# Block inverses in four parts instead of two; preparation of the filter stage moved into the projection

## The reference, cut to what matters

```
q, k, v = silu(causal 4-tap convolution of x @ W.T)           # 4 heads of 64
beta    = sigmoid(x @ Wb.T)
A       = strictly lower part of -(beta k)(k^T), in chunks of 32 tokens
T       = inverse(I - A)                                      # 32 x 32, 64 chunks x 4 heads x 4 batches
local_s, local_m, local_l = causal filters of v with 3, 15 and 63 taps
probs   = softmax((x @ gate_w + gate_b) / temp) * (1 - 5 eps) + eps     # 5 gates a head
o       = p0 local_s + p1 local_m + p2 local_l + p3 delta(q, k, v, T) + p4 v
```

## Time and profile before

| | us |
|---|---|
| median of three runs | 2339.09 (2338.53 to 2339.15) |
| the profiled execution | 2325.58 |
| its span | 2323.8 |
| projection | 0 to 359.15 |
| filter stage | 359.15 to 576.40 |
| delta stage and network | 576.40 to 2323.8 |

### The profile page before, as it was taken

One profiled execution on the slowest core, in us unless ns is written; L12 is line 12 of the kernel. 1 busy time (PEld: TensorE's weight loads), 2 busy tenths in 40 slices (PEclk: granted clock), 3 DMA queues, 4 the chain that ended last, 5 costly groups with the idle time before them and its releaser, 6 DMA issues.

```text
span 2323.8 us, 41398 instructions
## 1 busy us (share of the span) xinstructions
PE 2086.2 (90%) x16936; PEld 1766.6 (76%) x16936; DVE 1157.7 (50%) x1819; ACT 864.5 (37%) x1406; POOL 533.1 (23%) x563
## 2 busy tenths in 40 slices
PE   7888873776899888779999999999999999999998
PEld 5776763676777777658888888888888888888886
DVE  5777768963477767732343244234324323432332
ACT  4445541110233333234344344434434433443442
POOL 1112787875455554500000000000000000000000
PEclk9999996798799999989999999999999999999999
DMA  5766666776999999500000000000000000000000
GB/s 162 203 189 178 185 206 173 245 248 235 217 226 207 208 206 204 132 27 1 19 19 1 19 19 1 19 19 19 1 19 19 1 19 19 19 1 19 19 1 18
DMA packets 247007, 217.02 MB, mean 93 GB/s; under 512 B 159042, under 2 KB 210754, under 8 KB 242242
## 3 DMA queue, kind: packets, MB, share of 16 engines
q1 hardware_dynamic: 234562, 184.30, 31.0%
q10 hardware_dynamic: 12288, 30.41, 4.5%
HBM read 130.52 MB, written 84.15 MB: 92 GB/s over the span
## 4 chain that ended last, share of the span: by engine, by line
PE 55%; issue 1%; DVE 1%; ACT 1%; DMA 0%; POOL 0%; DVEq 0%; SPq 0%; ACTq 0%; POOLq 0%
PE B L1573 49%; PE O L1600 5%; PE T L1531 1%; DVE yb L1706 0%; ACT gate L1645 0%; DMA x<-x_s 0%; DVE stats L1737 0%; ACT L1645 0%; DVE z L1732 0%; DVE z L1728 0%; DVE xl L1686 0%; DVE z L1751 0%; ACT xh L1633 0%; POOL rstd L1787 0%; DVEq L1701 0%
## 5 line engine op out<-in xcount | busy, mean ns | idle before, releaser
L1573 PE MATMUL B<-act1l,wr 128*128 128x512 f32 x1024 | 398.5, 389 | 0.0
L1573 PE MATMUL B<-act0h,wr 128*128 128x512 f32 x1024 | 398.3, 389 | 0.0
L1573 PE MATMUL B<-act0l,wr 128*128 128x512 f32 x1024 | 398.3, 389 | 0.0
L1573 PE MATMUL B<-act1h,wr 128*128 128x512 f32 x1024 | 398.3, 389 | 0.0
L1659 ACT ACTIVATE yb<-B,scol 128x512 f32<-128x512 f32 x256 | 176.2, 688 | 581.1 <-PE B L1573 581.1
L1694 DVE TENSOR_TENSOR act0l<-yb,act0h 128x512 fp32r<-128x512 f32 x256 | 176.1, 688 | 378.0 <-ACT act0h L1662 375.8
L1784 POOL TENSOR_TENSOR rstd<-mv,ln_eps 128x4 f32<-128x4 f32 x16 | 3.2, 199 | 1303.5 <-DVE mv L1745 1303.5
L453 DVE SCALAR_TENSOR_TENSOR acc<-proj,taps,acc 128x512 f32<-128x512 f32 x288 | 214.7, 750 | 84.8 <-ACT acc L399 76.3
L1694 DVE TENSOR_TENSOR act1l<-yb,act1h 128x512 fp32r<-128x512 f32 x128 | 88.7, 693 | 295.4 <-ACT act1h L1662 295.4
L1573 PEld LDWEIGHTS B<-act0h,wr 128*128 128x128 f32 x1024 | 192.3, 188 | 39.9
L1573 PEld LDWEIGHTS B<-act1h,wr 128*128 128x128 f32 x1024 | 192.3, 188 | 39.9
(11 more groups left out here) (169 smaller groups left out, 3213.7 us busy)
## 6 DMA issues: line engine op xcount, KB each, us to landing
qk_s<-yT SPq DMA_DIRECT2D x16, 1024.0 KB, 6.2
kk_s<-kfull SPq DMA_DIRECT2D x16, 1024.0 KB, 6.4
qk<-qk_s SPq DMA_DIRECT2D x32, 512.0 KB, 6.5
wraw<-in_ffn_w ACTq DMA_DIRECT2D x32, 352.0 KB, 6.5
toe<-in_toe_short ACTq DMA_DIRECT2D x32, 320.0 KB, 7.4
xt<-in_xt SPq DMA_DIRECT2D x16, 524.0 KB, 4.3
k_s<-ktok SPq DMA_DIRECT2D x16, 512.0 KB, 7.2
v_s<-vtok SPq DMA_DIRECT2D x16, 512.0 KB, 3.2
```

The lines of the kernel that those rows point to most:

```text
L1573: last = nc.tensor.matmul(B[slot % 4][:, :], w, part, start=(k == 0 and i == 0), stop=(k == kts - 1 and i == len(parts) - 1))
```

## The change

The matrices are inverted in four parts of four steps each, two slots of `tri` a part. GpSimd does parts 0 to 2: part 0 in its iterations 6 to 9, part 1 in 10 to 13, part 2's columns 1 to 24 in 14 to 16 and the rest in the filter stage. VectorE does part 3 in the filter stage, 60 operations spread over groups 4 to 51. The scale tables of parts 0 to 2 are made behind steps 4, 8 and 12 and turned in steps 5, 9 and 13, and with them three quarters of the gates' softmax: logits behind steps 4, 8 and 12, shares behind steps 5, 9 and 13. The three engines' loops over steps are unrolled. The first head's windows are written from the value tile in each step, SBUF to SBUF; the first three band matrices are loaded at the program's start, and the zeros in them are set there. In the filter stage the remaining quarter is prepared, the first two convolutions come ahead of it, the softmax's table ahead of the block table, and the query scales behind the third weighing. The inverses leave in four parts, through two transposed tiles in turn.

```diff
-NSUB = GRP // P
-EARLY_STEPS = STEPS // NSUB
-
-EARLY_COLS = {10: (1, 5), 11: (5, 9), 12: (9, 12), 13: (12, 15), 14: (15, 18), 15: (18, 21), 16: (21, 25)}
+
+PARTS = 4
+PART_STEPS = STEPS // PARTS
+PSLOTS = SLOTS // PARTS
+PGRP = GRP // PARTS
+
+EARLY_COLS = {6: (0, 1, 8), 7: (0, 8, 14), 8: (0, 14, 20), 9: (0, 20, 31),
+              10: (1, 1, 8), 11: (1, 8, 14), 12: (1, 14, 20), 13: (1, 20, 31),
+              14: (2, 1, 8), 15: (2, 8, 15), 16: (2, 15, 25)}
 EARLY_END = 25
...
-    first = t * NS % P
+    c = t // PART_STEPS
+    if c >= 2 and t % PART_STEPS == 0:
+        queue.wait_ge(keep["tri_in"][c % 2], c // 2 * 16 * NQ * PART_STEPS)
     for q in range(NQ):
-        queue.dma_start(keep["tri"][first:first + NS, q * NSUB + t // EARLY_STEPS, :, :],
+        first = q // 2 * PGRP + t * NS % PGRP
+        queue.dma_start(keep["tri"][first:first + NS, c * PSLOTS + q % 2, :, :],
                         io["kk_s"][q * CH:q * CH + CH, t * NS:t * NS + NS, q * CH:q * CH + CH].rearrange("i n j -> n i j")
-                        ).then_inc(keep["tri_in"][t // EARLY_STEPS], 16)
+                        ).then_inc(keep["tri_in"][c % 2], 16)
+
+
+def blocks_there(engine, keep, c):
+    engine.wait_ge(keep["tri_in"][c % 2], (c // 2 + 1) * 16 * NQ * PART_STEPS)
...
+                    sp.dma_start(win0[:, NT + t * BATCH:NT + (t + 1) * BATCH, :], vtok[p][:, 0, :, :]).then_inc(v_stored[p], 16)
+                    sp.dma_start(win0[WIN:P, t * BATCH:(t + 1) * BATCH, :], vtok[p][0:WIN, 0, :, :]).then_inc(v_stored[p], 16)
+                    if t + 1 < STEPS:
+                        sp.dma_start(win0[0:WIN, (t + 1) * BATCH:(t + 2) * BATCH, :], vtok[p][WIN:P, 0, :, :]).then_inc(v_stored[p], 16)
...
-                    early = isinstance(t, int) and t == EARLY_STEPS + 1
+                    c = t // PART_STEPS - 1
+                    early = c in range(PARTS - 1) and t % PART_STEPS == 1
                     if early:
-                        pe.wait_ge(gam0_done, 1)
-                        nc.tensor.transpose(gam_ps, gam0[:, :, :, :].rearrange("p t r s -> p (t r s)"), ident).then_inc(gam0_turned, 1)
+                        pe.wait_ge(gam0_done, c + 1)
+                        turn_scales(nc, gam_ps, gam0, ident).then_inc(gam0_turned, 1)
                     turn(lambda hh, b: yT[p][:, KT + hh, b * P:b * P + P]).then_inc(ktok_ready, 1)
                     if early:
-                        pe.wait_ge(gam0_out, 2)
+                        pe.wait_ge(gam0_out, 2 * c + 2)
...
+                for t in range(STEPS):
...
+                for n in range(NTOE):
+                    toeplitz(act, io, keep, n)
+                act.wait_ge(prm_in, 16)
+                nc.scalar.activation(itemp[:, :], prm[:, NGATE:NGATE + HEADS], ACT.Exp, scale=-1.0).then_inc(itemp_done, 1)
...
+                for t in range(1, STEPS):
+                    step(t, t % 2, (t - 1) // 2, True, t < 2)
+                    if t % PART_STEPS == 0:
+                        c = t // PART_STEPS - 1
+                        act.wait_ge(small_out, t + 1)
+                        if c:
+                            act.wait_ge(gam0_done, c)
+                        nc.scalar.activation(ebeta[:, :, :], raw[:, c * NE:c * NE + NE, NGATE:NGATE + HEADS], ACT.Exp,
+                                             scale=-1.0).then_inc(exp0_done, 1)
+                        act.wait_ge(to_exp0, c + 1)
+                        nc.scalar.activation(lg0[:, :, :, :], lg0[:, :, :, :], ACT.Exp).then_inc(exp0_done, 1)
...
+                def first_logits(c):
+                    if c == 0:
+                        link(nc.vector.tensor_scalar(eps[:, :], prm[:, NGATE + HEADS:NGATE + 2 * HEADS], 0.0, 0.2, ALU.max, ALU.min))
+                        link(nc.vector.tensor_scalar(slope[:, :], eps[:, :], -5.0, 1.0, ALU.mult, ALU.add))
+                        dve.wait_ge(itemp_done, 1)
+                    dve.wait_ge(small_out, (c + 1) * PART_STEPS + 1)
+                    gate_logits(nc, link, keep, lg0, mx0, rows(c)).then_inc(to_exp0, 1)
+
+                def first_shares(c):
+                    dve.wait_ge(exp0_done, 2 * c + 2)
+                    link(gate_shares(nc, link, keep, lg0, mx0, rows(c)))
+
+                def first_scales(c):
+
+                    dve.wait_ge(kk_summed, (c + 1) * PART_STEPS + 2)
+                    nc.vector.tensor_scalar(ssk0[:, :, :].rearrange("p (t b) h -> p t (b h)", b=BATCH),
+                                            kk[:, c * PART_STEPS:(c + 1) * PART_STEPS, :], L2_EPS, None, ALU.add)
+                    dve.wait_ge(exp0_done, 2 * c + 1)
+                    link(nc.vector.tensor_scalar(ebeta[:, :, :], ebeta[:, :, :], 1.0, None, ALU.add))
+                    link(nc.vector.tensor_tensor(half0[:, :, :], ssk0[:, :, :], ebeta[:, :, :], ALU.mult))
+                    link(nc.vector.reciprocal(half0[:, :, :], half0[:, :, :]))
+                    if c:
+                        dve.wait_ge(gam0_turned, c)
+                    by_matrix(nc, gam0, half0[:, :, :]).then_inc(gam0_done, 1)
...
+                    if t % PART_STEPS == 0:
+                        first_logits(t // PART_STEPS - 1)
+                        first_scales(t // PART_STEPS - 1)
+                    if t % PART_STEPS == 1 and t > 1:
+                        first_shares(t // PART_STEPS - 1)
...
+                        c, first, end = EARLY_COLS[t]
+                        sub = Substitution(nc.gpsimd, keep, c, keep["outer0"])
                         if first == 1:
...
+                            pool.wait_ge(gam0_out, 2 * c + 2)
+                            pool.wait_ge(keep["sub_link"], c * SUB_LINKS + 1)
                             sub.scaled_columns().then_inc(keep["sub_link"], 1)
...
+                            pool.wait_ge(keep["sub_link"], c * SUB_LINKS + 2)
                             sub.ones_on_diagonal()
...
+                        early_columns(pool, sub, keep, c, first, end)
+                        if end == CH - 1:
+                            early_rows(pool, sub, keep, c)
+                    if t % PART_STEPS == 1 and t > 1:
+                        c = t // PART_STEPS - 1
+                        if c < PARTS - 1:
+                            blocks_there(pool, keep, c)
+                            Substitution(nc.gpsimd, keep, c, None).zero_above().then_inc(keep["sub_link"], 1)
...
+SUB_LINKS = 2 + 2 * (CH - 2)
...
+def early_columns(pool, sub, keep, c, first, end):
     for j in range(first, end):
...
+        pool.wait_ge(keep["sub_link"], c * SUB_LINKS + 2 * j)
         sub.outer_product(j).then_inc(keep["sub_link"], 1)
...
+        pool.wait_ge(keep["sub_link"], c * SUB_LINKS + 2 * j + 1)
         sub.update(j).then_inc(keep["sub_link"], 1)
+
+
+def early_rows(pool, sub, keep, c):
+    pool.wait_ge(keep["sub_link"], (c + 1) * SUB_LINKS)
+    sub.scaled_rows().then_inc(keep["inv_done"][0], 1)
+
+
+def gate_logits(nc, link, keep, lg, mx, rows):
+
+    temp = bcast(bcast_mid(keep["itemp"][:, :], rows.stop - rows.start), 5)
+    link(nc.vector.tensor_tensor(lg[:, :, :, :].rearrange("p t h f -> p t (h f)"), keep["raw"][:, rows, 0:NGATE],
+                                 bcast_mid(keep["prm"][:, 0:NGATE], rows.stop - rows.start), ALU.add))
+    link(nc.vector.tensor_tensor(lg[:, :, :, :], lg[:, :, :, :], temp, ALU.mult))
+    lgf = lg[:, :, :, :].rearrange("p t h f -> p (t h) f")
+    link(nc.vector.tensor_reduce(mx[:, :], lgf, AX.X, ALU.max))
+    return nc.vector.tensor_tensor(lgf, lgf, bcast(mx[:, :], 5), ALU.subtract)
+
+
+def gate_shares(nc, link, keep, lg, mx, rows):
+
+    n = rows.stop - rows.start
+    lgf = lg[:, :, :, :].rearrange("p t h f -> p (t h) f")
+    link(nc.vector.tensor_reduce(mx[:, :], lgf, AX.X, ALU.add))
+    link(nc.vector.reciprocal(mx[:, :], mx[:, :]))
+    by_head = mx[:, :].rearrange("p (t h) -> p t h", h=HEADS)
+    link(nc.vector.tensor_tensor(by_head, by_head, bcast_mid(keep["slope"][:, :], n), ALU.mult))
+    link(nc.vector.tensor_tensor(lgf, lgf, bcast(mx[:, :], 5), ALU.mult))
+    return nc.vector.tensor_tensor(keep["pw"][:, :, :, rows].rearrange("p h f t -> p t h f"), lg[:, :, :, :],
+                                   bcast(bcast_mid(keep["eps"][:, :], n), 5), ALU.add)
+
...
+def turn_scales(nc, out, gam, ident):
+
+    for rows in HALVES:
+        last = nc.tensor.matmul(out[rows, :], gam[rows, :, :, :].rearrange("p t r s -> p (t r s)"), ident[rows, rows],
+                                start=True, stop=True)
+    return last
...
+        OPS = 2 * (CH - 2)
+        SUB_END = 4 + OPS * 4 // 5
+
+        D_OUT, T_OUT = {2: 0, 6: 1, 12: 2, 28: 3}, {4: 0, 8: 1, 14: 2, 29: 3}
+
+        TURNS = {2: 0, 5: 1, 11: 2, 27: 3}
...
+                pe.wait_ge(keep["toe_zero"], NTOE)
                 convolve(0)
                 convolve(1)
+                pe.wait_ge(gam_done, 1)
+                turn_scales(nc, gam_ps, gam, ident).then_inc(gam_turned, 1)
...
```

(102 more changed lines are left out.)

218 lines of the change are left out of this document (57 added, 161 removed).

## The result

The changed kernel takes 2390.66 us (median of 4 runs, 2377.91 to 2398.22); the kernel before took 2338.81 (4 runs, 2328.75 to 2339.15). The ratio is 1.0227, interval 1.0175 to 1.0279: 52 us slower, where 13 us faster were forecast. On the two chips used further down the kernel before took 2324.61 and 2323.91 us, so kernels are compared by their ratio to it on the same chip. The profiled execution took 2389.58 us, with a span of 2387.6.

The account below looks back on a forecast made before the run. Bounds: in projection a TensorE, ScalarE and VectorE loop; in the heads VectorE (first), DMA (third), TensorE's pace (fourth). Projection +39 and filter stage -52 gave -13 us, so 2326 us; range 2303 to 2344.

Parts of the forecast that it names:

- The inverses' 6.3 MB leave in four parts: Filter stage heads: two parts leave in head 1, one each in heads 2 and 4, priced at 311 GB/s.
- points at steps 4, 8, 12: Projection: three preparation points on VectorE instead of one, with waits for GpSimd at 8 and 12; about +13 us.
- turns and shares, 5, 9, 13: Projection: scale tables turned in three steps instead of one (+6), softmax ended behind the last convolution (+6); about +12 us.
- GpSimd late, steps 10 and 14: Projection: GpSimd some 5 us late at the squares VectorE awaits, 0.8 us each; 1.5 us in all.
- tail: Projection's end: ten columns instead of four follow GpSimd's last key squares, and the stage waits for them; +11.5 us.
- the lock: Steps 8 and 12: VectorE operations each wait for one GpSimd operation of about 1.1 us; 5.2 us of waiting a point.
- Preparation of the filter stage: Filter stage's start: softmax shrinks to a quarter, first weighing after 14 us instead of 35.7; about -21 us.
- The four heads: Filter stage after the first weighing: 36 + 40.5 + 33.5 + 32.5 = 142.5 us against 174.2; about -31 us.
- (b): Filter stage: transfers don't scale with bytes, window bursts ahead of filter matrices stall TensorE; 2345 us, chance 0.10.
- (a): Projection from step 6 on: GpSimd becomes the pace, seen at squares of steps 10, 14 and the end; 2356 us, chance 0.14.
- (c): Projection: preparation points cheap, no lock at steps 8 and 12, GpSimd ends 8 late; +18, 2305 us, chance 0.16.
- (d): Filter stage: transfers give way, heads run at TensorE's pace of 28.2 us; 2298 us, chance 0.10.

Follow-up runs that it names:

- the split version: The changed kernel with each of its twelve 512 KB inverse stores issued as two, 64 rows outermost: 2307.13 us, ratio 0.993; run again 2309.06 us, ratio 0.9928.
- the quiet version: The split version with GpSimd's columns moved out of steps 8 and 12 to the steps beside them: 2304.06 us, ratio 0.9926.

## Why the prediction was wrong

**The failed step: "The inverses' 6.3 MB leave in four parts ... At 311 GB/s".** I priced the stores by bytes at the rate of all sixteen engines. They ran on two, at 53 GB/s. Forecast for the stage 165 us, measured 250.8; with the stores on sixteen engines 169.1. Of the 86 us between forecast and result 82 go with the form of these stores alone. The diff had all that was needed: `"q n (i j)"` puts a size of two outermost. I looked at bytes and piece sizes, which had not changed, and not at the shape.

**Projection, +39 forecast, +30.85 measured.** Token loads after (SyncE, start and length), the ones around steps 8 to 10:

```profile
188.34 0.35 SPq L235 DMA_DIRECT2D xt<-in_xt  x1
215.12 0.35 SPq L235 DMA_DIRECT2D xt<-in_xt  x1
236.80 0.35 SPq L235 DMA_DIRECT2D xt<-in_xt  x1
257.76 0.35 SPq L235 DMA_DIRECT2D xt<-in_xt  x1
```

| term | forecast | measured, from the token loads unless said |
|---|---|---|
| start | +3 | +3.75 (first product 13.45 against 9.70) |
| points at steps 4, 8, 12 | +13 | +12.5: 22.26, 26.78 and 26.38 us against 3 x 20.3, less 2.0 |
| turns and shares, 5, 9, 13 | +12 | +2.7: 23.20, 21.68, 21.67, less the 3.0 of before |
| GpSimd late, steps 10 and 14 | +1.5 | +1.3: 20.96, 20.97 (the latter from the v_s stores) |
| tail | +11.5 | +12.0: GpSimd ends 18.5 us behind the last v_s store (371.44 to 389.96), before 6.5 |
| unrolled loops | -2 | about -1: a plain step is 20.18 and no longer alternates |

The one term that is far off is the turns and shares: at steps 9 and 13 they cost 1.4 us each and not 5.5. The table is one trace, though. In the second trace of the split version, whose projection has the same code, the steps at the points took 23.87, 27.75 and 26.51 us and those of the turns 23.22, 25.05 and 21.65, so by it the points cost 15.2 and the turns and shares 6.0. Even there the latter are half the forecast. That GpSimd's end closes the projection was right, and the length of its tail from the fit over sizes came out within half a microsecond.

At steps 8 and 12 the sum was right and its parts were not. VectorE's gap is 6.25 us (200.06 to 206.31), not 8.5, and the quiet version's is 3.5 (204.60 to 208.12): the point's own work is about the 3.3 of the forecast, and the lock 2.7 instead of 5.2. The rest came from TensorE. Its timeline in the changed kernel at step 8, then a stretch behind the point, and one behind the same point in the second trace of the split version:

```profile
206.12 1.36 PE L331 MATMUL side<-yT 64*128 64x128 f32 x16 [3.97 <-ACT kfull L407]
208.67 3.86 PE L293 MATMUL proj<-xt,w_qkv 128*128 128x262 f32 x8 [1.19 <-DVE acc L470]
```

```profile
207.00:213.00 6.00, 4.82 (x24) 3.25 (x22) 3.71 (x6) 3.43 (x5) 0.00 (x0) 0.50 0.00 0
```

```profile
209.00:221.00 12.00, 10.94 (x80) 8.87 (x81) 5.72 (x10) 3.90 (x6) 3.48 (x2) 0.50 0.20 50
```

TensorE has no work for 3.97 us, until 206.12. From 207 its granted clock is 0.50, the lower of its two levels (1.2 and 2.4 GHz), and it is back at 1.00 in the slice that begins at 214. The eight products that took 2.03 us at 200.12 take 3.86 at 208.67. I had no term for that. In the second trace the pause is the same (3.98 us) and the lower level lasts for more than 12 us, although TensorE is busy for 10.94 of them; the next step, which begins at that level, is 25.05 us long where it was 21.68. A tensor-by-scalar operation does wait for GpSimd, as the prediction took it to (1.09 us against 0.19), but for less than a whole GpSimd operation, and the next one, at 204.03, not at all (0.18 against 0.20). The rule that I took this from (the Trainium skill, SBUF — State Buffer, Who interferes with whom) agrees with these rows; my price of it was too high.

**Preparation of the filter stage, -21 forecast.** Right: 12.4 us to the first weighing, where 14 was said and 11 to 20 allowed.

**The four heads, -31 forecast.** With split stores the heads take 34.2, 40.9, 43.7 and 29.8 us (first weighing at 402.46, then the rows of that kernel), forecast 36, 40.5, 33.5 and 32.5: 148.5 for 142.5. The second term that was mis-sized is the third head. It was to fall from 42.87 to 33.5 us because an inverse's bytes leave it, and it stayed: 11.9 MB at 273 GB/s (273 x 43.65) where 10.2 MB at 311 was forecast. The second trace has 44.1 us at 270 GB/s. Why full engines moved less there is open.

So with split stores the two stages come to +31 and -48, or -17 us, in the first trace and to +36 and -46, or -10, in the second; the timed ratio of 0.993 is -16 us, and I had said -13. The first trace as a whole is 28 us shorter than that of the kernel before, but 11 of these lie in the later stages, whose code is the same. The number would have been near by luck in part: the projection was 8 us cheaper in that trace than forecast and the third head 10 us dearer. The idea of the change held for a kernel that this one was not.

**The rivals.** (b) was nearest: the transfers don't scale with bytes, a burst stalls TensorE. But its mechanism (windows ahead of filter matrices, 2345 us) is not what cost the 82 us; a head as long as its 42.9 us did come with split stores, but only one, the third (43.7). (a) fell where it was priced, since steps 10 and 14 were no later than forecast; in the last steps GpSimd is indeed full, and there its length was in my sum. (c) was right in that the lock was cheap, but the points still cost 12.5 us and GpSimd's tail 12.0. (d) fell, with split stores: heads 2 and 3 stand at 40.9 and 43.7 us with full DMA engines. No rival had a transfer that is confined to a part of the engines, so the range ended 47 us too low.

## What to carry to other kernels

For each transfer that a change reshapes, write down the outermost size of both of its sides before its bytes: with the same 4 KB pieces an outermost size of two ran at 53 GB/s and four at 105, and with 64 the low plateau was gone and the stage 82 us shorter. In a trace, look for stretches where a DMA share stands still at a low value and the rate with it while nothing else runs: 0.13 here. Such a store also holds up other work: every transfer with a share on its engines, and every issue behind it in its queue, waits. Here each of the twelve lengthened the stage by 6.6 to 7.3 us. Four to six microseconds in the projection could be argued over for a page, and one `rearrange` outweighed them all.

Before a step's length is explained from one trace, look at a second one of the same kernel: here one ended its projection 5 us later than the other.

## What the hardware showed that I had not expected

- A store on two engines delays transfers that have all sixteen: the stage's last 2 MB store landed 24.8 us after its issue behind such stores and 6.3 us without them. SyncE's queue was held for up to 15 us at a 512 KB issue.
- A full DMA share does not fix the rate: 0.99 went with 316 GB/s in one head and 1.00 with 273 in the next.
- A pause of TensorE inside a busy step was followed by the lower clock in one execution and not in another of the same kernel. At step 4 the split version pauses for 3.31 us in both of its traces; in the first the clock stayed at 1.00 and the eight products behind it took 2.03 us, in the second it fell to 0.50 and they took 3.25 (22.26 and 23.87 us for the step). At step 8, after a pause of about 4 us, it fell in both, for some 7 us in one and for more than 12 in the other. What decides that stayed open.
